# A decoder layer's attention on one core: means, squares, variances, inverses and query-head turns in other steps of the unit, x statistics in pieces, key scores ahead of projections where a batch begins

## What is computed

```python
kv = _ln(x, kvn_w, kvn_b) @ kv_w + kv_b            # k, v: 16 heads of 32
q = (_ln(x, qn_w, qn_b) @ q_w + q_b).reshape(b, c, HEAD, HD).transpose(0, 2, 1, 3)
q, k = _rotary(q, x, rh_w, rh_b), _rotary(k, x, rh_w, rh_b)   # radius from x @ rh_w
qn, kn = _ln(q, ln_w, ln_b), _ln(k, ln_w, ln_b)    # over the 32 of a head
scores = jnp.einsum('bhqd,bhkd->bhqk', qn, kn) / np.sqrt(HD).astype(np.float32)
attn = jax.nn.softmax(scores, axis=-1)
a = jnp.einsum('bhqk,bhkd->bhqd', attn, v)
return a.transpose(0, 2, 1, 3).reshape(b, c, dims) @ out_w + out_b
```

## Time and profile before

| | |
|---|---|
| median of 3 runs | 2026.33 us (2024.2 to 2029.24) |
| the profiled execution | 2028.34 us, span 2026.5 us |
| PE busy | 1771.1 us, 87% of the span |
| DVE, ACT, POOL busy | 1477.8, 1260.5, 867.1 us |
| mean granted TensorE clock | 0.95 of full speed |

### The profile page before, as it was taken

One profiled execution on the slowest core, in us unless ns is written; L12 is line 12 of the kernel. 1 busy time (PEld: TensorE's weight loads), 2 busy tenths in 40 slices (PEclk: granted clock), 3 DMA queues, 4 the chain that ended last, 5 costly groups with the idle time before them and its releaser, 6 DMA issues. The chain is left out here.

```text
span 2026.5 us, 26481 instructions
## 1 busy us (share of the span) xinstructions
PE 1771.1 (87%) x8648; PEld 1333.6 (66%) x8648; DVE 1477.8 (73%) x2915; ACT 1260.5 (62%) x2674; POOL 867.1 (43%) x802
## 2 busy tenths in 40 slices
PE   6788888988889888898878999999997999999972
PEld 5556665666656666566535888888786777777751
DVE  7768688686876868767655777777764688888876
ACT  3388677787877878777784322222224667777764
POOL 3678668676786767867630222222220000000000
PEclk9799999999999999999978999999998999999986
DMA  4222132321423213222144011111112011111111
GB/s 153 56 80 63 47 110 62 95 64 40 117 62 96 63 46 111 63 73 63 54 144 151 20 54 53 63 63 63 63 59 72 22 42 63 63 63 63 42 42 63
DMA packets 86184, 141.06 MB, mean 70 GB/s; under 512 B 16544, under 2 KB 19616, under 8 KB 86048
## 3 DMA queue, kind: packets, MB, share of 16 engines
q1 hardware_dynamic: 86048, 139.37, 22.7%
HBM read 63.82 MB, written 25.17 MB: 44 GB/s over the span
## 5 line engine op out<-in xcount | busy, mean ns | idle before, releaser
L526 DVE TENSOR_REDUCE a_neg_max<-a_max 128x1 fp32r<-128x512 f32 x512 | 340.6, 685 | 150.5 <-PE a_max L911 148.3
L796 ACT ACTIVATE a_probs<-a_exp 128x512 f32<-128x512 f32 x512 | 294.4, 606 | 206.2 <-PE a_exp L929 205.1
L775 ACT ACTIVATE a_max<-a_max,a_neg_max 128x512 f32<-128x512 f32 x512 | 346.7, 688 | 13.2 <-DVE a_neg_max L526 11.8
L911 PE MATMUL a_max<-a_stack 96*128 96x512 f32 x512 | 220.5, 457 | 85.6 <-ACT a_max L775 77.7
L368 POOL TENSOR_TENSOR a_rstd<-a_rstd,a_minus_half 128x16 f32<-128x16 f32 x64 | 185.9, 2905 | 96.5 <-DVE a_rstd L510 96.4
L886 PE MATMUL a_t<-a_w_hi,a_zT_hi 128*128 128x384 f32 x500 | 183.9, 368 | 36.4 <-DVE a_v L491 27.8
L911 PEld LDWEIGHTS a_max<-a_stack 96*128 96x128 f32 x512 | 99.3, 197 | 175.2 <-ACT a_max L775 130.4
L1717 POOL TENSOR_TENSOR f_yrstd<-f_yrstd,f_minus_half 128x4 f32<-128x4 f32 x8 | 11.0, 1376 | 473.5 <-DVE f_yrstd L1736 473.5
L929 PE MATMUL a_exp<-a_stack 100*128 100x512 f32 x512 | 191.7, 416 | 9.7 <-ACT a_probs L796 6.5
L887 PE MATMUL a_t<-a_w_lo,a_zT_hi 128*128 128x384 f32 x500 | 176.3, 353 | 0.0
L888 PE MATMUL a_t<-a_w_hi,a_zT_lo 128*128 128x384 f32 x500 | 176.1, 352 | 0.0
(11 more groups left out here) (282 smaller groups left out, 4823.6 us busy)
## 6 DMA issues: line engine op xcount, KB each, us to landing
a_stack<-a_nT_hi SPq DMA_DIRECT2D x512, 64.0 KB, 2.0
a_stack<-a_nT_lo SPq DMA_DIRECT2D x256, 64.0 KB, 2.0
a_z<-x SPq DMA_DIRECT2D x8, 1024.0 KB, 7.8
a_y<-x SPq DMA_DIRECT2D x8, 1024.0 KB, 5.6
r_xn<-x SPq DMA_DIRECT2D x8, 1024.0 KB, 5.5
r_cn<-ctx SPq DMA_DIRECT2D x8, 1024.0 KB, 7.8
x<-r_xn SPq DMA_DIRECT2D x16, 512.0 KB, 2.8
f_xn<-x SPq DMA_DIRECT2D x8, 1024.0 KB, 5.5
```

The costliest lines, as they stand in the source:

```text
L526: nc.vector.tensor_reduce(neg_max[:, t, ROW + h:ROW + h + 1].bitcast(F32R), bank_max[i % NB][:, :], AX_X, ALU.max, negate=True).then_inc(m ...
L775: nc.scalar.activation(bank_max[i % NB][:, :], bank_max[i % NB][:, :], ACT.Exp, bias=neg_max[:, t, ROW + h:ROW + h + 1], accum_out=sums[:, ...
L796: nc.scalar.activation(probs[:, kt % 2, h, :], bank_exp[i % 2][:, :], ACT.Exp).then_inc(exp_done, 1)
L911: mm(bank_max[i % NB][:, :], stack[0:ROW, par, h, t * P:(t + 1) * P], stack[0:ROW, par, HG + h, :], start=True, stop=True).then_inc(score_ ...
```

## The change

Steps of the tables move, and a few lines with them. `head_mean` of both sides stands at step 14 of the unit before (side 1 stood at step 0). `square` is at steps 0 and 1 in place of 1 and 2 and ahead of the exponentials, `head_var` behind steps 0 and 1 in place of 2 and 3, `invert` behind step 2 in place of 6, `save_inverse` at 14 in place of 12 except in g=3. In g>0 the query side turns at step 9 in place of 10, with the banks of the projection swapped to suit. `x_stats` is cut in two parts at four steps. On POOL `add_bias` stands behind `centre`, and `x_rstd` between the rotations. In g=0 the key scores are further ahead, and each goes before a projection item; `weigh` follows. z's first high and low parts are a step earlier, and projections of g=1 wait for z's tiles one by one.

```diff
-KS_DONE = tuple(min(4 * (i + 1) // 3, T * HG) for i in range(16))
+KS_DONE = ((2, 5, 7, 8, 9, 10, 11, 12, 13, 14, 15, 16, 16, 16, 16, 16),
+           tuple(min(4 * (i + 1) // 3, T * HG) for i in range(16)))
-WEIGH_AT = (5, 7, 10, 13)
+WEIGH_AT = ((3, 5, 9, 13), (5, 7, 10, 13))
-Z_AT, Z_HIGH_AT, Z_LOW_AFTER = (12, 12, 13, 13), (13, 13, 14, 14), (13, 13, 14, 14)
+Z_AT, Z_HIGH_AT, Z_LOW_AFTER = (12, 12, 13, 13), (12, 13, 13, 14), (12, 13, 13, 14)
-VAR_AFTER, SQUARE_AT = (2, 3), (1, 2)
-TURN_HIGH_AT, TURN_LOW_AFTER = ((9, 12), (9, 11)), ((10, 13), (10, 12))
-INVERT_AFTER, INVERSE_AT, INVERSE_SAVE_AT, ATTN_HIGH_AT, ATTN_LOW_AFTER = 6, 11, 12, 0, 0
+VAR_AFTER, SQUARE_AT = (0, 1), (0, 1)
+TURN_HIGH_AT, TURN_LOW_AFTER = ((9, 12), (9, 10)), ((10, 13), (10, 11))
+INVERT_AFTER, INVERSE_AT, INVERSE_SAVE_AT, ATTN_HIGH_AT, ATTN_LOW_AFTER = 2, 11, (14, 14, 14, 12), 0, 0
...
@@ POOL, unit
                 if left >= 2:
                     for s in range(2):
                         centre(U + 2, s)
+                if g >= 2:
+                    for t in range(2 * (g - 2), 2 * (g - 1)):
+                        add_bias(b, t)
+                if left >= 2:
                     for s in range(2):
                         head_norm(U + 2, s)
+                if left >= 3:
+                    rotate(U + 3, 0)
                 if g == 3 and more:
                     x_rstd(b + 2)
                 if left >= 3:
-                    for s in range(2):
-                        rotate(U + 3, s)
-                if g >= 2:
-                    for t in range(2 * (g - 2), 2 * (g - 1)):
-                        add_bias(b, t)
+                    rotate(U + 3, 1)
...
@@ DVE, unit
                     if i == SAVE_MAX_AT and left >= 3:
-                        head_mean(U + 3, 0)
+                        for s in range(2):
+                            head_mean(U + 3, s)
...
@@ PE, key_scores
                 if i < 2:
+                    if U % G == 1 and U < G * (B - 1):
+                        pe.wait_ge(zlo_done, T * (U // G + 1) + 3 + i)
                     pe.wait_ge(maxrow_saved, 2 * U + i + 1)
...
@@ PE, project_item
-                    if m == 0 and g == 1:
-                        pe.wait_ge(zlo_done, T * (b + 2))
+                    if g == 1:
+                        pe.wait_ge(zlo_done, T * (b + 1) + t + 1)
...
@@ PE, unit
+                    items = list(within(PROJECT_DONE, i)) if left >= 3 else []
+                    keys = list(within(KS_DONE[g > 0], i))
+                    if g > 0 or i == 0:
+                        for m in items:
                             project_item(b, g, m)
-                    for m in within(KS_DONE, i):
-                        key_scores(U, g % 2, m)
+                        for m in keys:
+                            key_scores(U, g % 2, m)
+                    else:
+                        for n_item in range(max(len(items), len(keys))):
+                            if n_item < len(keys):
+                                key_scores(U, g % 2, keys[n_item])
+                            if n_item < len(items):
+                                project_item(b, g, items[n_item])
```

More of the change, by code:

```diff
@@ L435, in _, with x_variance @@
             dve.wait_ge(split_done, 1)
-            def x_stats(b, t):
+            def x_variance(b, t):
                 if t == 0:
@@ L441, in x_stats @@
                 nc.vector.bn_stats(stats[:, t, :], z[:, t, :])
+            def x_stats(b, t):
                 nc.vector.scalar_tensor_tensor(scratch[:, :], z[:, t, :], 1.0, rh_w[:, :], ALU.mult, ALU.mult,
@@ L594, in unit @@
                         next_lower(*SPLITS[SPLIT_AT.index(i)])
-                    if left >= 2 and i == 0:
-                        for s in range(0 if U == 0 else 1, 2):
+                    if U == 0 and i == 0:
+                        for s in range(2):
                             head_mean(U + 2, s)
@@ L612, in unit @@
                     if g >= 2 and more and i in STATS_AFTER:
-                        x_stats(b + 2, 2 * (g - 2) + STATS_AFTER.index(i))
+                        t, half = divmod(STATS_AFTER.index(i), 2)
+                        (x_stats if half else x_variance)(b + 2, 2 * (g - 2) + t)
                     if g == 3 and more and i == FINAL_AFTER:
@@ L701, in _ @@
             for t in range(3):
+                x_variance(1, t)
                 x_stats(1, t)
@@ L713, in _ @@
                 save_qkv(1, 1, t, bank_t[t % 2])
+            x_variance(1, 3)
             x_stats(1, 3)
@@ L816, in unit @@
                             sum_exps(U + 1, (g + 1) % 2, m)
-                    for m in within(KS_DONE, i):
+                    for s in range(2):
+                        if left >= 2 and i == SQUARE_AT[s]:
+                            square(U + 2, s)
+                    for m in within(KS_DONE[g > 0], i):
                         exps(U, m)
@@ L820, in unit @@
                         attn_hi(U - 1, (g - 1) % G)
-                    if i == INVERSE_SAVE_AT:
+                    if i == INVERSE_SAVE_AT[g]:
                         save_inverse(U)
                     for s in range(2):
-                        if left >= 2 and i == SQUARE_AT[s]:
-                            square(U + 2, s)
                         if left >= 2 and i == TURN_HIGH_AT[g > 0][s]:
@@ L963, in project_item @@
                 if k == 0:
-                    if m == 0 and g == 1:
-                        pe.wait_ge(zlo_done, T * (b + 2))
+                    if g == 1:
+                        pe.wait_ge(zlo_done, T * (b + 1) + t + 1)
                     if t < one:
-                        if t == 1:
+                        if t == 0 and one == 2:
                             pe.wait_ge(nTlo_done, 2 * (U + 1) + 2)
@@ L974, in project_item @@
                         pe.wait_ge(qkv_saved, T * (U + 3) + t + 1 - one)
-                project(U + 3, (g + 3) % G, t, k, bank_t[t % one])
+                project(U + 3, (g + 3) % G, t, k, bank_t[0 if g == 0 else (t + 1) % 2])
             def turn_item(b, g, left, s):
@@ L1015, in unit @@
                             query_scores(U + 1, (g + 1) % 2, m)
-                    if left >= 3:
-                        for m in within(PROJECT_DONE, i):
+                    items = list(within(PROJECT_DONE, i)) if left >= 3 else []
+                    keys = list(within(KS_DONE[g > 0], i))
+                    if g > 0 or i == 0:
+                        for m in items:
                             project_item(b, g, m)
-                    for m in within(KS_DONE, i):
-                        key_scores(U, g % 2, m)
-                    if i in WEIGH_AT:
-                        weigh(U, g, WEIGH_AT.index(i))
+                        for m in keys:
[6 more added lines that the diff above has]
+                                project_item(b, g, items[n_item])
+                    if i in WEIGH_AT[g > 0]:
+                        weigh(U, g, WEIGH_AT[g > 0].index(i))
                     if left == 0 and OUT_PART_AT <= i < OUT_PART_AT + T * (G - 1):
```

8 lines of the change are left out of this document (4 added, 4 removed).

## The result

The changed kernel took 2041.81 us (median of 20 runs, 2022.44 to 2048.56), beside 2026.37 us for the kernel before (20 runs, 2022.92 to 2031.28). The ratio is 1.0063 with a 95% interval of 1.0047 to 1.008. It is slower, where 1988 us was forecast, and above the range of 1968 to 2016. Its runs lie in two groups that overlap nowhere: 5 of 20 at 2022.4 to 2026.0 us, with a mean granted clock of 0.940 to 0.948, and 15 at 2038.8 to 2048.6, with 0.930 to 0.934. The profiled execution (2040.7 us) is one of the second group, so the profile shows that group alone.

A forecast was written before the change was run, and what follows sets the result against it. No engine was taken as full: four engines wait for each other in a ring, read where PE stands still. Terms of 2.8, 1.1, 1.2 and 0.3 us sum to 5.4 a batch, 39 in all, giving 1988 us, range 1968 to 2016.

The forecast's parts named there:

- (a): Start of g=0: means at the unit's end and earlier variances let projection item 4 start sooner; 2.8 us a batch.
- fourth rival: Ends of units: DVE waits for POOL's late rotation in front of the maximum; slower, 2043 us, chance 0.09.
- The clock: Start of g=0: 12 matmuls ran at the lower clock behind PE's idle time, 1.5 us more; expected to stay up.
- the sign that was named: Start of g=0: idle before the projection falls from 2.68 to under 1.3 us, and the 12 matmuls step at 0.18.
- (b): End of g=0: PE's waits for z's low parts, 1.35 and 0.98 us, go; 1.1 us a batch in all.
- (e): g=0: keys ahead of projections, weights sooner, query side turned a step sooner; costed at 0, as part of (a).
- (c): ACT in g=1, 2, 3: squares fill idle time before the first keys, inverse's copy moves later; 1.2 us a batch.
- (d): End of g=2: bias additions moved away from DVE's cast and scaling of the mean; 0.3 us a batch.
- third rival: Ends of g=2 and g=3: POOL's centre blocks DVE's cast, normalisation 1.05 us late; 2003 us, chance 0.12.
- second rival: All units: POOL becomes the bound, so only (a) stays; 2007 us, chance 0.20.
- The x statistics: DVE passes of 512 columns, only spread over four steps in place of two, no instruction added; no cost counted.

The follow-up runs named there:

- e9: Changed kernel with the variances alone back behind steps 2 and 3, squares still early: 2005.64 us, ratio 0.9894 to the kernel before.
- e12: e9 with the inverses also back at their old step, behind step 6: 1996.01 us, ratio 0.9847 to the kernel before.
- e4: Kernel before with only the key scores of g=0 further ahead and the weights with them: 2020.03 us, ratio 0.9968.
- e16: e12 with the means as before too (side 1 at step 0): 2011.3 us, ratio 0.9915 to the kernel before.
- e5: Changed kernel with squares and variances at their old steps, both means still at the unit's end: 2010.31 us, ratio 0.9909 to the kernel before.
- e1: Changed kernel with x's moments behind step 12 in place of 9 and x's root behind both rotations: 2033.37 us, ratio 1.0043 to the kernel before.
- e13: e12 with the part on x's statistics as before: 2005.92 us, ratio 0.9887 to the kernel before.
- e15: Kernel before with only the squares and variances moved early: 2042.09 us, ratio 1.0071.
- e6: Changed kernel with only the means as before (side 1 at step 0): 2039.58 us, ratio 1.0062 to the kernel before.

## Why the prediction was wrong

**The failed step** is the one in term (a) on the variances: "head_var is now behind attn_low instead of two row steps later", 3.1 us sooner for POOL, and nothing against it. The prediction followed the released engine and named nothing queued behind the two reductions on DVE. Behind them stood the first row maximum, and its lateness goes through ACT's exponentials to PE's score bank. The sooner pow itself was worth little: e9 gives it back (its first pow in g=3 starts 4.9 us or more behind the normalisation) and is 36 us faster than the change. Together with the same omission for `invert` (which the prediction did not cost at all) it is 46 us: 36 for the variances (e9 against the change) and 10 for the inverses (e12 against e9), more than the whole gain of 39 that was forecast. The fourth rival had the right form, DVE work in front of a maximum, but another maximum (the spread at the unit's end), another cause (waiting for POOL) and the chance 0.09. In the change DVE's means don't wait for POOL at all, and in e12, the faster kernel, they do, 18.5 us in 16 times. That the rival gave 2043 us is a coincidence.

**The clock** was priced at one place, the 12 matmuls at the start of g=0, and was counted only as something to win. It is also something to lose. In the changed kernel the waits became 26 us shorter in sum, and 38 us of busy time came on top, nearly all of it in the four stretches at the lower clock: in the batch of the rows they are 13 us longer than before, and PE is busy 7 us longer. One of them stands behind the new 1.55 us; the other three are at the ends of g=1, 2 and 3, and what makes them longer or new is not shown. In the batches of the rows those three are 16.6 us in the change, 13.7 with the variances undone (e9) and 3.5 with the inverses undone too (e12).

Point by point:

- (a), the start of g=0. POOL's chain is shorter, by less than forecast. The first pow starts at 321.51, 3.9 us behind the normalisation at 317.6, where 3.1 was forecast and 4.7 was before, and POOL's wait for it is 1.50 us where under 1 was forecast.

```profile
321.51 2.91 POOL L369 TENSOR_TENSOR a_rstd<-a_rstd,a_minus_half 128x16 f32<-128x16 f32 x1 [1.50 <-DVE a_rstd L516]
...
342.15 0.72 POOL L355 TENSOR_TENSOR a_n<-a_turn 128x256 f32<-128x256 f32 x1
```

 The last rotation ends at 342.87, 25.3 us behind that normalisation, against 27.3 before. PE's wait for the save is gone and the step before and behind item 4 is 0.18:

```profile
348.34 0.33 PE L899 MATMUL a_t<-a_w_hi,a_zT_lo 128*128 128x384 f32 x1
348.52 0.63 PE L942 MATMUL a_exp<-a_stack 100*128 100x512 f32 x2
349.75 0.47 PE L942 MATMUL a_exp<-a_stack 100*128 100x512 f32 x1 [0.60 <-ACT a_probs L806]
350.06 0.34 PE L897 MATMUL a_t<-a_w_hi,a_zT_hi 128*128 128x384 f32 x1
```

 So the sign that was named came, but not by the move that the term rests on, the mean of side 1 ahead of the normalisation. With the mean left where it was the wait for the save goes from 19.9 us to 5.3 by the keys ahead alone (e4), and in e16, keys ahead and mean as before, it is 3.6, with the same 0.60 us before the third key and the step of 0.18. That the keys would fill the wait was in the term; that they suffice was not. And PE entered the stretch late and at the lower clock (0.32 at 347.11 and 347.43), and the unit takes 42.8 us, not 39 to 40. Without the variances and inverses it takes 41.1 to 42.8 (e12, first six batches).
- (b), z. The 1.35 us before the third transposition should go, with 0.6 before the fourth. The wait is now before the fourth and as long: 7.9 us in six times, 1.3 at most, where it was 8.1 in six. The second, 0.98 us before the projections (5.9 us in six times), is gone from the list. That is one half of the mechanism; 1 us a batch was forecast, and about that came. Its time was not measured apart.
- (e), the keys ahead, costed at 0 beyond their share in (a), are worth 6.6 us alone (e4), and the shorter wait for the save is theirs.
- (c), squares into ACT's idle time. e5 and e9 differ in the squares alone: 2010.31 and 2005.64 us, whose ratios overlap (0.989 to 0.9929, 0.9882 to 0.9907). By the ratios that is 3 us, and it can't be told from nothing; 8 in all was forecast. What the inverse's later copy on ACT gives was not measured apart. That the inverses' reciprocal and spread enter DVE's queue ahead of the second maximum was the cost, and was missed.
- (d), the bias additions. At the end of g=2, where the cast took 1.73 us and the scaling of the mean 1.19, the cast now reads:

```profile
316.26 1.35 DVE L538 CAST a_stack<-a_stack 4x1024 fp32r<-4x1024 f32 x1 [0.33 <-ACT a_stack L798]
```

 So the turns with POOL became shorter and did not go: 0.66 us on the cast, once a batch (1.32 to 1.37 in seven of eight), 0.82 at the ends of g=1 and g=3. That is the third rival, at a third of its price. The second rival is out: POOL still waits 80.1 us for variances, where it waited 78.9. In e12 the same casts take 0.69 in all batches but one.
- The x statistics were costed at nothing. In g=3 they make PE wait 2.21 us, by the turns that small DVE operations take with POOL. In e1, without that wait, 8 us come back; on e12 the same part gains 10 (e13). The Trainium skill (SBUF — State Buffer, Who interferes with whom) says that a DVE tensor_scalar can enter a mode that contends with GpSimd, and that whoever issues first then blocks the other for its whole instruction. The trace agrees: the tensor_scalar at 335.77 takes 0.79 us and ends at 336.56, just behind a product of POOL's that ran from 335.79 to 336.54; its like at 336.60, issued ahead of POOL's next one at 336.62, takes 0.17. Which of the first two issued first can't be told from 0.02 us between their starts. The third rival took that rule to the cast; it bit harder at the moments.

What stays open: how much of the 36 us is clock and how much lateness can only be read from single executions (19.9 and 16.3); what makes the stretches at the lower clock at the ends of units; and why 5 of 20 executions of the changed kernel keep the time of the kernel before. They have the higher mean clock, but none of them was profiled. Where the means' 15 us come from was not followed on the trace beyond PE's busy time (18.6 us less in e12 than in e16, the fastest execution of one beside the slowest of the other).

## What to carry to other kernels

When a step is moved forward, list what now stands behind it on its own engine, and follow that to the engine that waits, before counting what it releases. Here two steps of 1.7 us that only feed an engine with slack (POOL had 79 us of waits) cost 36 us where they went ahead of one that frees a bank for PE. When a wait is gone, undo the parts one at a time before one of them gets the credit: the mean's move had it here, and the keys ahead did it. When several parts are changed together, try each on the version without the worst one: parts that looked worthless here (means, x statistics) were worth 10 to 15 us in the version without the worst ones.

## What the runs showed of the hardware

A wait of PE can cost more than its length, because the matmuls behind it may run at the lower of the two levels, and its length doesn't tell whether they will. PE kept the higher one behind 0.91 us (before) and 1.12 us (e15) at the start of g=1, and lost it behind 1.55 us (the change) in six of seven units, but not in the first. Behind 1.30 to 1.33 us (e6) it lost it in one of seven. At the ends of units it lost it behind 1.14 us in the change and kept it behind 1.14 in e12, and kept and lost it behind 1.63 in the kernel before. PE was busy 1767 us with the matmuls of e12 and 1810 us with those of the change, 42 us apart, at granted clocks of 0.957 and 0.934. The changed kernel's executions lie in two groups with nothing between 2026.0 and 2038.8 us, whose medians are 19 us apart. And of the operations on 128 x 4 elements beside POOL's rotation one took 0.17 us and three 0.39 to 0.79, while one of POOL's products took 1.06 in place of 0.74.
